# The rotary multiply by the sines on GpSimd, without a wait for the item's scores

## The reference

```python
def _rope(x, sin, cos):
    xe = x[..., ::2]
    xo = x[..., 1::2]
    re = xe * c - xo * s
    ro = xe * s + xo * c
    return jnp.stack((re, ro), axis=-1).reshape(x.shape)

def _attn(xq, ctx, wq, wkv, wo, bo):
    q = _heads(xq @ wq)
    k, v = jnp.split(ctx @ wkv, 2, axis=-1)
    k = _heads(k)
    v = _heads(v)
    q = _rope(q, sq, cq)
    k = _rope(k, sk, ck)
    sim = jnp.einsum('bhnd,bhmd->bhnm', q, k) * DH ** (-0.5)
    a = jax.nn.softmax(sim, axis=-1)
    o = jnp.einsum('bhnm,bhmd->bhnd', a, v)
    o = o.transpose(0, 2, 1, 3).reshape(xq.shape[0], xq.shape[1], MID)
    return o @ wo + bo
```

## Time and profile before

| | |
|---|---|
| median of 3 runs | 393.87 us (393.54 to 394.5) |
| profiled execution, its own time | 393.85 us |
| span of that execution, first to last instruction | 392.1 us |
| TensorE busy | 375.7 us, 96% |
| VectorE busy | 305.3 us, 78% |
| ScalarE busy | 293.4 us, 75% |
| GpSimd busy | 177.5 us, 45% |
| granted TensorE clock, mean over the span | 0.995 of full speed |

### The profile page before, as it was taken

One profiled execution on the slowest core, in us unless ns is written; L12 is line 12 of the kernel. 1 busy time (PEld: TensorE's weight loads), 2 busy tenths in 40 slices (PEclk: granted clock), 3 DMA queues, 4 the chain that ended last, 5 costly groups with the idle time before them and its releaser, 6 DMA issues.

```text
span 392.1 us, 9870 instructions
## 1 busy us (share of the span) xinstructions
PE 375.7 (96%) x3591; PEld 287.5 (73%) x3591; DVE 305.3 (78%) x657; ACT 293.4 (75%) x1022; POOL 177.5 (45%) x156
## 2 busy tenths in 40 slices
PE   7999999999999999999999898999999999999997
PEld 3577777777877777777787577776768778788665
DVE  4779978979888888787898668674758888888751
ACT  2377878878878788777877585789679887987942
POOL 3165547557456665445575224342465650402120
PEclk9999999999999999999999899999999999999999
DMA  7153343223333333332122100000000000000001
GB/s 250 51 181 128 111 131 109 101 83 109 123 120 110 109 110 108 109 114 96 55 82 83 54 30 26 2 2 0 3 2 2 2 3 2 2 2 3 4 0 54
DMA packets 17424, 26.09 MB, mean 67 GB/s; under 512 B 3584, under 2 KB 6272, under 8 KB 17376
## 3 DMA queue, kind: packets, MB, share of 16 engines
q1 hardware_dynamic: 17088, 25.24, 19.0%
q10 hardware_dynamic: 288, 0.22, 0.3%
HBM read 8.67 MB, written 0.52 MB: 23 GB/s over the span
## 4 chain that ended last, share of the span: by engine, by line
PE 71%; DVE 15%; ACT 8%; issue 3%; POOL 2%; DMA 1%; DVEq 0%; POOLq 0%
PE bank L984 57%; PE bank L1065 7%; PE bank L1272 5%; ACT prob L437 3%; DVE nmax L847 2%; ACT raw L523 2%; DVE hT L668 1%; DVE nmax L719 1%; POOL xn L282 1%; DVE st L641 1%; DVE qk L751 1%; PE bank L1311 1%; PE bank L995 1%; DVE xn L656 1%; DVE x L636 1%
## 5 line engine op out<-in xcount | busy, mean ns | idle before, releaser
L301 POOL TENSOR_TENSOR swp<-swp,small 128x512 f32<-128x512 f32 x62 | 78.4, 1279 | 48.1 <-PE bank L984 28.3
L437 ACT ACTIVATE prob<-bank,nmax 128x128 f32<-128x128 f32 x256 | 91.5, 391 | 1.2 <-DVE nmax L719 1.2
L523 ACT ACTIVATE raw<-bank,nmax 128x128 f32<-128x128 f32 x256 | 72.7, 390 | 11.0 <-DVE nmax L847 10.9
L719 DVE TENSOR_REDUCE nmax<-bank 128x4 f32<-128x512 f32 x64 | 41.2, 685 | 29.7 <-PE bank L984 29.7
L437 ACT ACTIVATION_READ_ACCUMULATOR prob<-bank,nmax 128x1 f32 x256 | 59.2, 231 | 0.0
L334 POOL TENSOR_TENSOR prob<-prob,rz 128x512 f32<-128x512 f32 x29 | 30.2, 1041 | 55.1 <-DVE rz L724 55.1
L847 DVE TENSOR_REDUCE nmax<-bank 128x4 f32<-128x512 f32 x64 | 41.2, 684 | 15.4 <-PE bank L984 15.4
L984 PE MATMUL bank<-hT,wqkv 128*128 128x512 f32 x96 | 49.2, 596 | 0.5 <-DVE qk L751 0.5
L443 ACT ACTIVATE probT<-bank 128x512 f32<-128x512 f32 x32 | 19.1, 597 | 35.3 <-PE bank L1065 35.3
L751 DVE TENSOR_TENSOR qk<-bank,small 128x512 f32<-128x512 f32 x64 | 42.8, 670 | 0.9 <-ACT raw L428 0.6
L984 PEld LDWEIGHTS bank<-wqkv,oT 128*128 128x128 f32 x256 | 33.2, 192 | 14.0 <-issue 12.9
(11 more groups left out here) (114 smaller groups left out, 665.9 us busy)
## 6 DMA issues: line engine op xcount, KB each, us to landing
swp<-raw SPq DMA_DIRECT2D x124, 128.0 KB, 2.1
wqkv<-in_wqkv SPq DMA_DIRECT2D x16, 256.0 KB, 2.8
wff<-in_wff SPq DMA_DIRECT2D x4, 256.0 KB, 3.0
x<-in_x SPq DMA_DIRECT2D x2, 256.0 KB, 4.1
wmod<-in_wmod SPq DMA_DIRECT2D x1, 512.0 KB, 6.0
rows<-in_row SPq DMA_DIRECT2D x2, 192.0 KB, 2.4
ctx<-in_ctx SPq DMA_DIRECT2D x1, 384.0 KB, 3.1
ctxT<-in_ctxT SPq DMA_DIRECT2D x1, 384.0 KB, 3.4
```

Of the source, the lines that this page charges most:

```text
L301: nc.gpsimd.tensor_tensor(four(swp[:, m % 2, f, :]), four(swp[:, m % 2, f, :]), sin[f], ALU.mult).then_inc(rope_sin[f], 1)
L437: last = nc.scalar.activation(prob[:, hh, bcols(u)], S[hh][:, bcols(u)], ACT.Exp, bias=nmax[:, s % 2, hh, u:u + 1], accum_out=zsum[:, s % ...
L523: last = nc.scalar.activation(prob1[:, s % 2, hh, bcols(u)], score_bank(s, hh)[:, bcols(u)], ACT.Exp, bias=nmax[:, s % 2, hh, u:u + 1])
L719: nc.vector.tensor_reduce(nmax[:, s % 2, hh, :], four(S[hh][:, :]), AX.X, ALU.max, negate=True).then_inc(rowmax[hh], 1)
```

## The change

One wait is taken out of GpSimd's slot. In slots 0 to 29 GpSimd no longer waits for the scores of the slot's item before it multiplies by the sines. What is left before the multiply is the wait for the landing of the swaps, and the place behind `normalise_second`.

```diff
             def l0_slot(s):
                 if 1 <= s <= 29:
                     normalise_second(s - 1)
-                if 0 <= s < ITEMS - 2:
-                    pool.wait_ge(scores[0], s + 1)
                 if 1 <= s + 1 < ITEMS - 1:
                     rope_sine(s + 1, 0)
                     rope_sine(s + 1, 1)
                 background0(s)
```

## The result

The changed kernel takes 397.36 us (median of 5 runs, 396.79 to 400.08) where the kernel before takes 393.87. The ratio is 1.009, with a 95% interval of 1.0061 to 1.0118: slower by 3.5 us. A second measurement, beside other experiments, gave 1.0082 (1.0055 to 1.0109). The forecast was 394.2 us with a range to 395.8, so both the size and the forecast of "within 0.3%" were wrong.

The account below looks back on a forecast made before the run. The prediction took TensorE to bound the kernel (work in 96% of the span, 71% of the chain). From 393.85 us, -0.35 for slot 28 and +0.7 for slot 7's L690 gave 394.2 us, range 393.2 to 395.8.

Parts of the forecast that it names:

- within 0.3%: Whole kernel: no change a measurement can tell, about 0.3% or 1.2 us; chance of "same" 0.74.
- -0.35 us for slot 28: Slot 28: k multiply and bias add L312 move up 0.35 us, so L713 on the chain ends that much sooner.
- 0 for the four L690 of slot 16: Slot 16: delay costs 0 us, as TensorE has two projections more and about 0.9 us of spare time.
- first step: Slot 7: one q multiply splits the four L690, row maximum 1.04 us late, 0.39 spare; costs +0.7 us.
- second step: L656 pairs: q multiply asks too late to get in before the second L656; cost taken as 0 us.
- rival C: L656 pairs: GpSimd wins there too, six pairs cost 1.05 us on top, 395.25 us; chance 0.22.
- Rivals A: VectorE's groups: not split, the multiply waits them out, only slot 28 changes; 393.5 us, chance 0.25.
- D: Waits before L301: the removed wait was never last, swap landings slip everywhere; time unchanged at 393.85 us, chance 0.08.
- E: Five slots with bias add L312: each frees 0.35 us, 1.75 us in all, 392.1 us; chance 0.05.
- The rival worked out beside the rule of the Trainium skill: The same as rival C: by issue order alone, the multiply queued ahead blocks the second L656; chance 0.22.

Follow-up runs that it names:

- slot 8 alone: Kernel before with the wait for the scores taken out of slot 8 only: 395.7 us, ratio 1.0045 to the kernel before.
- the pairs alone: Kernel before with the wait taken out only of the eight slots behind a pair of L656: 394.81 us, ratio 1.0019.
- the run with slot 8 free and odd rows: Kernel before without slot 8's wait, the context's norm reading rows of 3 x 32 from a padded tile: 395.05 us, ratio 1.0006.
- the run with the wait in ten slots: Kernel before with the wait kept in the ten slots behind VectorE's groups, gone from the other twenty: 395.18 us, ratio 1.0013.
- the run that waits for the groups: Kernel before with GpSimd waiting in ten slots for VectorE's group end instead of the scores, no wait elsewhere: 394.05 us, ratio 0.9994.

## Why the prediction was wrong

*Right:* the wait removed stood in front of work that nobody waits for; ordinary slots neither gain nor lose (ratio 1.0013); the q multiply follows L334 at once where its swap has landed; from the group of slot 7 the chain goes through ScalarE's exponentials to the context's scale and shift. The danger was named: VectorE's groups, in the right ten slots.

*Right in part by chance: -0.35 us for slot 28, and 0 for the four L690 of slot 16.* In slot 28 of the changed kernel L711, the L713 of before, isn't held any more (0.23 us instead of 1.18), but L312 came 0.6 us earlier against the slot's row maxima, not 0.35, and now holds the instruction before it (L710, the L712 of before: 0.81 us instead of 0.19). The two together are 0.3 us shorter, and TensorE waits 1.59 us instead of 1.92. In slot 16 the group wasn't met at all, for the q multiply began 0.8 us after its end, when its swap landed:

```profile
138.80 1.41 DVE L688 TENSOR_SCALAR ctx<-ctx,mv_c,rstd_c 128x96 f32<-128x96 f32 x4
```

```profile
141.02 2.50 POOL L301 TENSOR_TENSOR swp<-swp,small 128x512 f32<-128x512 f32 x2 [1.59 <-DMA swp<-raw]
```

The spare time of TensorE, by which the prediction came to 0, wasn't tried there.

*Wrong, first step: "The multiply gets in behind the first or second and holds the rest" (+0.7 us for slot 7's four L690).* I let GpSimd take one turn in the group. It takes one between any two VectorE instructions, as long as it has one ready: L334, q, k and L312 held one L690 each. The group grew by 3.0 us, not by 1.0, and slots 7 to 9 by 3.2 us in the first profile of the whole change, 4.7 in the second (with a stretch at 1.2 GHz), 1.8 with slot 8 alone. The earlier trace rows showed the rule (a waiting GpSimd instruction gets in between two) and I applied it once. I also left out that the k multiply may follow for the next turn, and L312 behind it. The row of 2.50 us for two multiplies in the earlier trace rows shows k's swap landed by 73.4 us; whether it would be in time 1.3 us after an early q multiply it does not say, and the runs went both ways.

*Wrong, second step: "I take 0" for the pairs of L656.* The race was lost: in six of the eight pairs, as rival C had it, the second L656 is held for one multiply, 1.94 us for the pair instead of 0.96. Rival C priced that at 1.05 us, 0.9 of it behind slot 9; the column grows by 1.1 us from item 10 to 29, by 1.15 in the second profile and by 0.7 with the pairs alone. So the price was about right, and what kept rival C's 395.25 us too low was in the main slot 8. Slot 3, with 0.9 us instead of 0.15, is not the pair's alone: L728 takes 1.62 us there beside a k multiply that had waited 2.40 us for its swap to land.

```profile
36.59 1.94 DVE L654 TENSOR_SCALAR xn<-x,mv,rstd 128x128 f32<-128x128 f32 x2
...
41.04 1.62 DVE L728 TENSOR_TENSOR prob<-prob,rz 128x512 f32<-128x512 f32 x1
```

```profile
40.84 1.28 POOL L301 TENSOR_TENSOR swp<-swp,small 128x512 f32<-128x512 f32 x1 [2.40 <-DMA swp<-raw]
```

In the run with slot 8 free and odd rows, whose slot 3 is that of the kernel before, the same instruction (there L732) was held as well, and its column grows by 0.4 us there:

```profile
41.37 1.58 DVE L732 TENSOR_TENSOR prob<-prob,rz 128x512 f32<-128x512 f32 x1
```

*Missing:* small instructions with one tensor input meet GpSimd too. L648 (128x4) took at most 0.30 us before, and the same line lasts 0.97 in slot 10 of the changed kernel, behind an L312 that came earlier. And the clock: after waits of TensorE of 1 to 2 us there are stretches at 1.2 GHz in part of the runs, about 1.5 us each, which no sum of instructions holds. They explain little of the loss: in the second measurement 8 of 12 runs of the changed kernel had one or two, and 22 of 35 of before. The rival worked out beside the rule of the Trainium skill, SBUF — State Buffer, section "Who interferes with whom" (issue order decides) was the better guide for the pairs; the prediction gave it 22%.

*A reading that was off.* By the earlier trace rows L730 ends at 91.38 us, 0.55 us after L312's end at 90.83 and not 0.11. That the two exclude each other stands: the last 0.69 us of L730, its usual time, begin 0.14 us before L312's end.

*Rivals A, D and E* are shut out: VectorE does not keep its run, the wait was last in 26 of 40 places, and freed L730 brought nothing.

## What to carry to other kernels

A wait that costs an idle engine nothing may be what keeps it off another engine's path: before it is taken out, list which instructions of the other engine the earlier work will run beside, and count one hold for each pair of them, not one for the group. A run of short VectorE instructions from SBUF to SBUF, in the form that L690 and L656 have, was the worst neighbour here for a GpSimd queue without gaps, since every one of them may wait for a whole GpSimd instruction; in another form (rows of 3 x 32) it was none. The better lever here was a single GpSimd instruction on the path's wrong side, moved by one slot.

## What the hardware showed that I had not expected

- Four VectorE `tensor_scalar` of 128x96, 1.2 us of work, took 4.36 us beside four GpSimd instructions in a row: turns are taken one by one, in both profiles of the change.
- The same four with a source of 3 x 32 rows took 0.36 us each instead of 0.32 and were never held.
- How early a held VectorE instruction gets going depends on that instruction and not on GpSimd's: if its usual time is counted back from its end, L688 and L654 begin 0.25 us before the recorded end of the one they wait for, be it L334, L301 or L312, and L728 and L646 0.14 us before it (both profiles of the change).
- A wait of TensorE of 1.9 us in a kernel that keeps it 96% busy was followed by 3.4 us at 1.2 GHz in some executions and not in others (the run with the wait in ten slots had it, the run that waits for the groups had not, both with 1.9 us of idle time). In slot 8 the two profiles of the change differ in the same way, each with 2.25 us of work in the 4 us before. What decides between the two stays open. The stretches behind the wait, the run with the wait in ten slots first, then the run that waits for the groups (stretch, busy times, granted clock):

```profile
223.00:227.00 4.00, 4.00 (x23) 2.69 (x22) 1.28 (x3) 0.26 (x2) 3.22 (x3) 0.64 0.08 27
```

```profile
221.00:225.00 4.00, 4.00 (x26) 2.40 (x27) 1.63 (x3) 1.59 (x4) 2.87 (x3) 1.00 0.10 37
```

The one is granted 0.64 on the mean of 4 us, the other the full 2.4 GHz.
